# Two feed-forwards of a hybrid layer stack: GpSimd's and ScalarE's order in the second pipeline step

## The reference, cut to what matters

```python
x = x + attn_a(layernorm(x))      # Nystroem attention with a convolution, x is (2, 2048, 128)
x = x + ffn(layernorm(x), ...)    # feed-forward 0
x = x + attn_b(layernorm(x))      # linear attention, 16 heads of 8
x = x + ffn(layernorm(x), ...)    # feed-forward 1, same weights

def fp4_quant_dequant(x):         # blocks of 16 along the last dimension
    scale = maximum(max(abs(xb)) / 6, 1e-12)
    return GRID[searchsorted(MID, abs(xb / scale))] * sign(xb) * scale

def ffn(x):                       # w_gate, w_up: (352, 128); w_down: (128, 352)
    gate, y = fp4_linear(x, w_gate), fp4_linear(x, w_up)
    h = silu(gate) * y            # (4096 tokens, 352)
    return fp4_linear(h, w_down)
```

## Time and profile before

| | us |
|---|---|
| median of 3 runs | 637.01 (636.86 to 640.54) |
| the profiled execution | 637.31 |
| its span, first to last instruction | 635.6 |
| PE busy in the span | 577.8 (91%) |
| DVE busy | 487.4 (77%) |
| ACT busy | 361.4 (57%) |
| POOL busy | 303.3 (48%) |
| mean granted TensorE clock | 0.984 of full speed |

### The profile page before, as it was taken

How to read it: one execution, slowest core, us unless ns; L and a number is a source line. 1 busy time by engine, 2 the same in 40 slices (tenths; PEclk the granted TensorE clock), 3 DMA queues, 4 the chain that set the end, 5 groups by cost and what they waited for, 6 DMA issues and landing times.

```text
span 635.6 us, 14058 instructions
## 1 busy us (share of the span) xinstructions
PE 577.8 (91%) x5407; PEld 426.2 (67%) x5407; DVE 487.4 (77%) x1004; ACT 361.4 (57%) x679; POOL 303.3 (48%) x351
## 2 busy tenths in 40 slices
PE   4889998799999999987999988999999988599997
PEld 3777887466666679964777765656656655377776
DVE  6978888466666664887999876778778786889975
ACT  5643322344444443157998774556556557699975
POOL 6542111122223223546788677255554435667763
PEclk9999999799999999998999999999999999999999
DMA  9500000000000001000000000000000000000101
GB/s 248 135 2 1 3 2 2 1 1 1 2 1 2 1 3 35 2 0 1 1 2 2 1 1 1 3 2 2 2 2 2 1 3 2 1 18 18 34 18 51
DMA packets 15942, 9.58 MB, mean 15 GB/s; under 512 B 1478, under 2 KB 15750, under 8 KB 15876
## 3 DMA queue, kind: packets, MB, share of 16 engines
q1 hardware_dynamic: 15876, 8.69, 5.1%
HBM read 6.59 MB, written 2.10 MB: 14 GB/s over the span
## 4 chain that ended last, share of the span: by engine, by line
PE 43%; DVE 23%; POOL 14%; issue 11%; ACT 8%; DMA 1%; SPq 0%; POOLq 0%; DVEq 0%; ACTq 0%
PE ps L1440 6%; PE ps L1597 4%; PE ps L1456 4%; PE ps L1614 4%; PE ps L1635 3%; PE ps L1743 3%; PE ps L1619 3%; DVE r L965 3%; POOL G L335 3%; DVE m L1016 3%; PE ps L1447 3%; ACT S L549 2%; POOL arena L429 2%; ACT qbd L578 2%; PE ps L1630 2%
## 5 line engine op out<-in xcount | busy, mean ns | idle before, releaser
L394 POOL TENSOR_TENSOR A<-S,r 126x512 f32<-126x512 f32 x36 | 38.0, 1057 | 147.6 <-DVE r L968 132.9
L429 POOL TENSOR_SCALAR_AFFINE_SELECT arena<-arena 128x1024 f32<-128x1024 f32 x32 | 35.9, 1121 | 65.6 <-ACT arena L802 65.5
L1614 PE MATMUL ps<-wguT,xnt 128*128 128x352 f32 x128 | 52.1, 489 | 8.1 <-ACT xnt L642 5.4
L335 POOL TENSOR_TENSOR G<-S,hoff 128x704 f32<-128x704 f32 x31 | 47.1, 1520 | 24.9 <-DVE S L1112 24.7
L1635 PEld LDWEIGHTS ps<-wdT,xnt 128*128 128x128 f32 x372 | 48.5, 191 | 8.2 <-ACT xnt L649 1.4
L1635 PE MATMUL ps<-wdT,xnt 128*128 128x128 f32 x372 | 51.9, 275 | 0.9 <-ACT xnt L649 0.9
L802 ACT ACTIVATE arena<-ps 128x1024 f32<-128x1024 f32 x32 | 32.7, 1022 | 33.9 <-PE ps L1743 33.9
L1280 DVE TENSOR_TENSOR arena<-ps,XN 128x1024 f32<-128x1024 f32 x32 | 39.2, 1224 | 14.8 <-PE ps L1743 14.8
L965 DVE TENSOR_REDUCE r<-S 126x16 f32<-126x512 f32 x36 | 24.7, 685 | 33.4 <-ACT S L549 33.4
L1619 PE MATMUL ps<-wguT,xnt 128*128 128x352 f32 x128 | 44.2, 469 | 0.0
L549 ACT ACTIVATE S<-S 126x512 f32<-126x512 f32 x36 | 22.5, 625 | 38.1 <-DVE S L960 38.1
(11 more groups left out here) (225 smaller groups left out, 1520.2 us busy)
## 6 DMA issues: line engine op xcount, KB each, us to landing
X<-in_x SPq DMA_DIRECT2D x8, 256.0 KB, 5.5
out<-X SPq DMA_DIRECT2D x7, 256.0 KB, 2.3
arena<-in_wqkvT SPq DMA_DIRECT2D x4, 256.0 KB, 5.4
band<-in_band SPq DMA_DIRECT2D x1, 897.8 KB
arena<-in_wqkvT SPq DMA_DIRECT2D x1, 512.0 KB, 7.7
early<-in_wfc SPq DMA_DIRECT2D x1, 512.0 KB, 9.4
kI<-in_scaled_eye SPq DMA_DIRECT2D x1, 192.0 KB
XN<-in_wattn SPq DMA_DIRECT2D x1, 192.0 KB, 2.4
```

The source lines that it names most:

```text
L335: tt(out=hgrid, in0=hmoved[k], in1=hoff[k][:, :], op=ALU.subtract).then_inc(s["fh_grid"], 1)
L394: tt(out=A1v[:, w % NW, :].rearrange("p (h m) -> p h m", m=M), in0=S1v[:, w % NW, :].rearrange("p (h m) -> p h m", m=M), in1=r1[:, 3, w % ...
L429: nc.gpsimd.affine_select(out=masked[n % 2][:, 8:16, :], in_=raw.rearrange("p (h t) -> p h t", t=P), pattern=[[0, 8], [1, P]], compare_op= ...
L1614: mm(ps[:, GATE_BANK, 0:F], xT[t // QD % 2][:, t % QD, :], wguT[:, 0:F], start=True, stop=True).then_inc(s["f_gate"], 1)
```

## The change

In step 1 of both feed-forwards GpSimd quantises h pair 0 before x group 2 instead of after it. ScalarE's activation of the seventh gate, silu(6), moves from the start of step 2 to step 1, in front of the offsets of h pair 1.

```diff
                 def step(r):                      # GpSimd
                     q = (r + FILL) // 2
+                    if r == 1:
+                        quantise_h(0)
                     if r % 2 and q < QN:
                         quantise_x(q)
-                    if 0 <= r - 1 < PN - p:
+                    if 1 <= r - 1 < PN - p:
                         quantise_h(r - 1)
...
-                    if 0 <= r + 1 < PN and r != 1:        # ScalarE
+                    if 0 <= r + 1 < PN and r not in (1, 2):
                         silu(2 * r + 2)
...
                     if r % 2 and q + 1 < QN:
                         normalise(q + 1)
+                    if r == 1:
+                        silu(6)
                     if 0 <= r < PN:
                         offset_h(r)
```

## The result

| | changed | before | |
|---|---|---|---|
| median of 6 runs each | 629.68 (626.7 to 631.72) | 636.93 (634.35 to 640.54) | 7.25 us faster |
| ratio | 0.9887 | | 95% interval 0.9858 to 0.9917 |
| profiled execution | 631.72 | 637.31 | |
| its span | 630.0 | 635.6 | |
| mean granted TensorE clock | 0.989 | 0.984 | |

The change makes the kernel faster, as forecast. It gained more than forecast (5.5), and the median lies 0.3 us under the range.

What follows compares the result with a forecast made beforehand. It took holes before both steady parts, where TensorE and VectorE waited on GpSimd's late h pair 0, as the removable loss. 2.9 + 2.6 = 5.5 us off the 637.01 median gave 631.5 us, range 630.0 to 634.3.

Steps and rivals of the forecast that it cites:

- signs of being wrong: gated(3) still waits for up matmuls, offset_h(1) ends after scale_x, or gated(4)-to-second-feed-forward-end distance changes beyond the second term.
- second term: Second feed-forward: GpSimd's new order brings gate(9) forward from 560.73 to 558.13; 2.6 us, bounds 0.1 and 3.2.
- The rival with one gain lost: One feed-forward's gain is given back at a later step decided by x: 634.2 us; chance 0.12.
- The silu edit at nothing: silu(6) before offset_h(1) gains nothing, as up(6) is bound by move_h(1); 0, with 0 to +0.9 us as price for both.
- cover of 0.5 us: Slack between offset_h(1)'s end and move_h(1)'s start, which hides silu(6); without it the move costs 0.46 us per feed-forward.
- First term: First feed-forward: GpSimd's new order ends VectorE's wait for up matmuls and brings gate(9) forward; 2.9 us, between 2.82 and 3.1.
- The link itself: ScalarE's chain from offset_x(3) through silu(8) sets gate(9), which starts 0.15 us behind silu(8)'s end.
- the first rival: ScalarE's chain does not decide last; TensorE shifts by 2.96 and 3.2 us: 6.2 to 7 us gained, 630.3; chance 0.16.
- The clock: TensorE's clock, 0.50 behind the hole before, was expected at 1.00 throughout; the sum needed no better clock.
- The slow rival: Several short holes make the clock dip in the second feed-forward's tensor-bound part; from the fourth dip slower, 638.4 us; chance 0.04.
- the dip of the earlier trace: In another stage, the clock fell to 0.91, then 0.66, despite TensorE in use; priced at 1.7 us of full clock.

Runs made afterwards that it cites:

- pe_order: Kernel before, GpSimd in old order; TensorE transposes h pair 0 after up(6), up(7), ScalarE copies it after offset_x(3): 634.93 us against 635.87, ratio 0.9973.
- pool_only: Changed kernel without the silu(6) move, GpSimd's new order alone: 631.30 us against 635.88 for the kernel before, ratio 0.9927.
- act_only: Kernel before with the silu(6) move alone, GpSimd in the old order: 635.29 us against 635.87, ratio 0.9987.
- dve_swap: Changed kernel with VectorE doing move_h(1) before scale_x(3) in step 2: 629.16 us against 635.87 for the kernel before; repeated, 630.60 against 635.65.
- before_fill: Kernel before with 16 unread matmuls in TensorE's wait in step 1 of both feed-forwards: 633.19 us against 635.87, ratio 0.9939.
- after_2: The changed kernel measured again beside the kernel before on one chip: 630.12 us against 635.88, ratio 0.9906.
- after_fill: Changed kernel with unread matmuls, 3 before gate(5) and 4 before the h transposes: 627.84 us against 635.65 for the kernel before, ratio 0.9885.

## Why the prediction was right in direction and in mechanism, and where it failed

*The cause and the place held.* h pair 0 waited in GpSimd's queue. Put first, it starts 0.15 us behind its release; of the waits of the earlier trace rows, VectorE's is gone in front of gated(3), and TensorE's is 0.2 us in the first feed-forward and 1.1 in the second. scale_x(3) waits for x group 2 as said (0.44 us in the second), and move_h(1) comes 0.57 later against move_h(0) (6.54 behind it, 5.97 before; the forecast had 0.6). None of the signs of being wrong came: gated(3) does not wait, offset_h(1) does not end behind scale_x, and from gated(4) to the end it is 1.4 us less (330.8 for 332.1), under the second term. pe_order shows that TensorE's queue alone was not the cause.

*The gain is kept.* What the first feed-forward won at 301 us (4.2 with the 1.1 won earlier) stands to 0.05 us up to 393 us. The rival with one gain lost is refuted; what was given back came behind that, in a stretch with a low clock that sits at 390 to 398 in this trace and at 396 to 400 in the other.

*The silu edit at nothing* held: pool_only has the same stretches, act_only the same second one. Its cover of 0.5 us was used up once, at the low clock of the changed kernel's first step 1, where offset_h(1) ends at 291.18 and move_h(1) starts at 291.21.

*First term, 2.9 forecast, 3.09 measured; second, 2.6 and 3.06.* Two sizes were off. The h pair's 3.12 us on GpSimd was read between two h pairs, but the second of them waits for its predecessor's result to be written (a count in `quantise_h`). An x group does not: x group 2 starts 2.94 behind (285.70 to 288.64) and 2.93 in the second. In the second, GpSimd's h pair also starts without a gap behind the moments. So offset_x(3) stands 8.71 and 8.70 us behind move_h(0), where the forecast had 8.75 and 8.98. The other size is the way from there to silu(8): 3.09 and 3.07 us, not 3.29 and 3.24. The old 3.50 held 0.41 us of waiting for TensorE and not 0.21: down_copy had also stood 0.09 for the down matmuls, and silu(8) comes 0.27 behind it, not 0.59. The link itself was right: gate(9) starts 0.14 to 0.15 us behind the end of silu(8) in every profile, and in dve_swap it moves by the 0.4 us that offset_x(3) moves. So the first rival, that ScalarE's link is not the last, is refuted, though its sizes of 2.96 and 3.2 lie closer to 3.09 and 3.06 than mine; that is luck.

*The step that failed is "The clock".* It said that the sum doesn't need a better clock, expected 1.00 throughout, and so put the clock at nothing. Both statements are wrong: the changed kernel's profile has 0.50 from 285 to 288 us, and before_fill shows 1.3 us of each stretch to be the clock, inside the terms. More, this part varies from one execution to another: the old order's stretch is 19.9 in the first profile and up to 21.1 in others, the new order's 16.8, or 17.6 to 17.8 where the clock falls in it. From the rows that gives, per stretch, 1.8 us of order, plus 1.3 to 2.5 of clock in the old order, less 0 to 1.0 in the new: 2.1 to 4.3, and 4.2 to 8.6 for both. The measured differences of 7.25, 5.8 and 5.6 lie in it. Outside the stretches, too, the time of unchanged code is not fixed: 281.1 to 285.8 us ahead and 238.5 to 241.2 between. The range was built only from the bounds of waits, all read in one execution, and left no room for either.

*The base.* The median of three runs, 637.01, was 1.1 above the median of the 67 runs of the kernel before on all chips, 635.87 (633.71 to 640.54); the changed kernel's 18 runs have 630.12. By these the gain is 5.75, near the forecast, and of the 1.8 us between 631.5 and 629.68 1.1 are in the base. That the gain is so near 5.5 is in part luck: in the two profiles of the first comparison the stretches gave 0.65 more than forecast, and the parts without an edit gave back 0.6 (1.1 gained ahead, 1.7 lost between), so that 631.72 us met the forecast of 631.8.

*The slow rival* supposed dips in the steady part. None came: the second feed-forward's steady part holds 1.00 up to its last 10 us in all the profiles of the new order. Nor did the dip of the earlier trace rows, priced at 1.7 us, cost the kernel before that much. It cost nothing: the changed kernel has 1.00 at that place (its 372 to 380 us), and its lead on VectorE is the same on both sides of the dip, 4.19 us at move_h (373.91 and 369.72) and 4.18 at a later instruction (394.30 and 390.12).

```profile
372.00:380.00 8.00, 5.17 (x34) 3.34 (x35) 4.72 (x12) 3.06 (x7) 7.24 (x12) 1.00 0.00 0
```

The Trainium skill, "TensorE: Matmul & The Clock Gate", section "A second HAM failure mode: psum-queue depth-cycling", holds that frequent short idle times can make the clock swing. The traces bear it out in the changed steps themselves (0.57 from 544 to 548 us in after_2, behind waits of 1.15, 1.12 and 1.25 us), where it cost up to 1.0 us, and not in the part that I had priced. They don't bear it out each time: behind waits of 1.14, 1.13 and 1.25 us the changed kernel's second stretch kept 1.00.

## What to carry to other kernels

Where one engine feeds two consumers, look up when each input was ready against when its turn came: a pair that is ready 1.4 us earlier and feeds the engine with the longest wait belongs first, even if the other group is then 1.6 to 1.7 us late. Measure such an edit between two fixed instructions on either side of it, in several profiles; here that told 0.4 us, while medians of whole runs disagreed by 1.7 us for the same pair of kernels. A long idle time of TensorE costs the wait and then the low clock behind it, and that second part should have a term and a spread of its own.

## What the runs showed of the hardware that I had not expected

The clock falls differently in executions of code that is the same up to that point. Ahead of step 1 of the first feed-forward the profiles differ by 4.7 us (move_h(0) at 285.79 in the kernel before, 281.07 in after_fill). Of this, 2.6 us arise from 118 to 129 us, where the clock is at 0.69 in the first and 1.00 in the second. TensorE's idle time in front is the same in both, 2.59 us.

The other 2.1 us arise in the first 25 us, at a clock of 1.00 in both. There one instruction of VectorE takes 3.7 us or 0.35, by whether a long one of GpSimd starts within 0.1 us of it or later. The kernel before, then after_fill:

```profile
20.92 3.72 POOL L380 TENSOR_TENSOR band<-band,late 126x1824 f32<-126x1824 f32 x1
...
21.01 3.72 DVE L871 TENSOR_SCALAR XN<-X,ln 128x128 f32<-128x128 f32 x1 [0.42 <-POOL ln L376]
```

```profile
20.88 0.35 DVE L875 TENSOR_SCALAR XN<-X,ln 128x128 f32<-128x128 f32 x1 [0.42 <-POOL ln L378]
...
21.17 3.73 POOL L382 TENSOR_TENSOR band<-band,late 126x1824 f32<-126x1824 f32 x1 [0.32 <-DMA late<-in_centre]
```

In nine of the fourteen profiles the two run side by side. In the other five GpSimd's has had to wait 0.3 to 1.6 us for its DMA, and the kernel is 1.0 to 2.2 us ahead of the kernel before's first profile from there on. No run was made to test this, so why VectorE's takes longer is not shown.

Matmuls that nobody reads, put into the old hole, kept the clock at 1.00 behind it and made the kernel 2.7 us faster although they add 7.5 us of TensorE work.
